# Layer 0's output projection: one FP32 product or three rounded products of high and low parts

## What is computed

```
h = gamma * layernorm(x) + beta                 # gamma, beta from the condition
q, k, v = split(h @ Wqkv.T + bqkv)
att = softmax(q @ k.T) / 512 ** 0.5             # per head, 1024 x 1024
out = (att @ v) @ Wp.T + bp                     # <- the projection, 1024 x 512 x 512 per batch
h1 = out + x
x1 = gamma * layernorm(h1) + beta + h1
```

## Time and profile before

| | |
|---|---|
| median of three runs | 2753.63 us |
| profiled execution, its own time | 2753.1 us |
| its span | 2750.3 us |
| PE busy | 2641.1 us, 96% |
| DVE, ACT, POOL busy | 2148.9, 1837.6, 1963.8 us |
| L997, the projection | 256 MATMULs, 117.3 us busy |
| mean granted TensorE clock | 0.988 of full |

### The profile page before, as it was taken

The page is one execution under the profiler, slowest core; times in us unless marked ns, Lnnn a source line. Parts: engine busy times, 40 slices in busy tenths (PEclk is TensorE's granted clock), DMA queues, the critical chain, the costliest instruction groups (busy, mean ns, idle before and its releaser), DMA issues. The chain is left out here.

```text
span 2750.3 us, 60608 instructions
## 1 busy us (share of the span) xinstructions
PE 2641.1 (96%) x22053; PEld 1488.5 (54%) x22053; DVE 2148.9 (78%) x4445; ACT 1837.6 (67%) x3315; POOL 1963.8 (71%) x1579
## 2 busy tenths in 40 slices
PE   9999999999999999999889999999999999998998
PEld 7655566555765547555445554554455445544443
DVE  5777678776787767877687778777877787758997
ACT  4466665666556665566556677667766776667996
POOL 0399844897459873689759887987889689965442
PEclk9999999999999999999989999999999999999999
DMA  7122353224432335223233214321432232245444
GB/s 238 40 60 59 118 171 105 59 60 151 139 98 59 80 124 170 72 60 105 79 80 82 60 33 120 83 59 36 114 79 60 58 90 60 60 171 178 104 104 111
DMA packets 170351, 260.46 MB, mean 95 GB/s; under 512 B 85436, under 2 KB 93252, under 8 KB 169160
## 3 DMA queue, kind: packets, MB, share of 16 engines
q1 hardware_dynamic: 168264, 250.27, 33.5%
q0 software_dynamic: 1792, 6.33, 0.6%
HBM read 99.15 MB, written 38.88 MB: 50 GB/s over the span
## 5 line engine op out<-in xcount | busy, mean ns | idle before, releaser
L555 DVE TENSOR_REDUCE a_mxs<-ps 128x1 f32<-128x512 f32 x2048 | 1268.6, 683 | 249.5 <-PE ps L420 247.1
L514 ACT ACTIVATE a_p<-ps 128x512 f32<-128x512 f32 x2048 | 1043.8, 605 | 196.7 <-PE ps L434 186.6
L374 POOL TENSOR_TENSOR a_sum<-a_p 128x512 f32<-128x512 f32 x736 | 939.1, 1286 | 196.5 <-PE ps L454 112.7
L420 PE MATMUL ps<-a_k,a_q 96*128 96x512 f32 x2048 | 853.1, 422 | 16.6 <-DVE a_mxs L555 14.6
L434 PE MATMUL ps<-a_q,a_k 98*128 98x512 f32 x2048 | 806.6, 418 | 15.8 <-ACT a_p L514 7.6
L454 PE MATMUL ps<-a_sum,a_unit 128*32 128x512 f32 x1536 | 650.5, 596 | 0.6 <-POOL a_sum L374 0.6
L380 POOL TENSOR_TENSOR a_sum<-a_sum,a_p 128x512 f32<-128x512 f32 x480 | 618.8, 1289 | 37.6
L454 PE MATMUL ps<-a_p,xv 128*32 128x512 f32 x3968 | 638.9, 595 | 0.0
L420 PEld LDWEIGHTS ps<-a_k,a_q 96*128 96x128 f32 x2048 | 386.2, 189 | 252.6 <-DVE a_mxs L555 101.5
L434 PEld LDWEIGHTS ps<-a_q,a_k 98*128 98x128 f32 x2048 | 383.3, 188 | 242.8 <-ACT a_p L514 145.4
L523 ACT ACTIVATE a_ots<-ps 128x512 f32<-128x512 f32 x256 | 152.8, 598 | 403.4 <-PE ps L454 402.3
(11 more groups left out here) (259 smaller groups left out, 3145.0 us busy)
## 6 DMA issues: line engine op xcount, KB each, us to landing
a_q<-qh SPq DMA_DIRECT2D x256, 128.0 KB, 2.3
a_k<-kh SPq DMA_DIRECT2D x256, 128.0 KB, 2.4
a_q<-ql SPq DMA_DIRECT2D x128, 128.0 KB, 2.4
a_k<-kl SPq DMA_DIRECT2D x128, 128.0 KB, 2.4
x<-a_p SPq DMA_DIRECT2D x64, 256.0 KB, 2.5
a_p<-in_w_fc SPq DMA_DIRECT2D x12, 1024.0 KB, 8.1
kh<-in_x SPq DMA_DIRECT2D x4, 2048.0 KB, 14.6
a_p<-x SPq DMA_DIRECT2D x16, 512.0 KB, 6.4
```

The lines of the kernel that those rows point to most:

```text
L374: pair = pool.tensor_tensor(tile, keys[0], keys[1], ALU.add)
L420: pe.matmul(self.mx[self.mx_ring[at]], self.q[j][0:96, t * P:(t + 1) * P], self.k[j][0:96, half * HALF:(half + 1) * HALF], start=True, sto ...
L514: act.activation(self.key_tile(u, kt), self.st[self.st_ring[CHUNKS * k + n]], ACT.Exp, scale=self.scale).then_inc(self.s_exp, 1)
L555: dve.reduce_max(self.mxs[:, k % 2, c:c + 1], self.mx[self.mx_ring[CHUNKS * k + c]], axis=AX.X).then_inc(self.s_mxr, 1)
```

## The change

The FP32 product is replaced by three F32R products (high token by low weight, high by high, low by high), 96 instead of 32 products a batch.

- ACT writes the rounded high part of all eight token groups (`HI_AT`, `high`), DVE subtracts it from PSUM and writes the low part (`LO_AT`, `low`). The low parts go into `q[0]`, `k[0]`, `q[1]`, `k[1]`, whose heads are over by then. These hold rows of ones that the next batch needs (`k[j][96:98]`), so POOL writes them again (`ones_rows`) at the head of each following batch and at the end of layer 0.
- The weight is split once, in batch 0, in head 14: four roundings on ACT, four subtractions on DVE (`WP_AT`). Both parts (2 MB) are written to DRAM behind batch 0's attention, and batches 1 to 3 load them in place of `wp` (2 MB for 1 MB).
- In `late()` the weight comes ahead of `h1`; `mod_r` and `bp` move to `after()`, into the free halves of `q[2]` and `k[2]`.
- SP gets four waits: `s_x1` ahead of the first loads of a batch, the end of head 14's scores in `after()`, `s_wplo` ahead of the write of the parts in batch 0, and, in the last batch, `s_y >= 32` ahead of the loads into `q[0]` and `q[1]`, since these now hold low parts until the projection is done.

```
@@ -142,6 +142,7 @@
     Pending.xq = nc.dram_tensor("xq1", [B, P, TT, D], BF16).ap()
     Pending.dq_row = nc.dram_tensor("dq1_row", [B, T], FP32).ap()
     Pending.dq_col = nc.dram_tensor("dq1_col", [B, P, TT], FP32).ap()
+    Pending.wp_parts = nc.dram_tensor("w0_proj", [P, 2 * KC * D], FP32).ap()
     Pending.w_hi = nc.dram_tensor("w0_hi", [P, 6, T], FP32).ap()
@@ -654,9 +657,12 @@
 
         late = [t[:, :, :].bitcast(FP32).rearrange("p k t -> p (k t)") for t in stage]
         wp = late[0][:, 0:KC * D].rearrange("p (k n) -> p k n", k=KC)
-        mod_r = late[0][:, KC * D:(KC + 2) * D].rearrange("p (i d) -> p i d", i=2)
-        bp = late[0][:, (KC + 2) * D:(KC + 3) * D]
-        oT = late[1].rearrange("p (k t) -> p k t", k=KC)
+        wp_parts = nc.alloc_sbuf_tensor_at("a_wp_parts", [P, 2, KC, D], F32R, offset=Pending.stage_at)
+        wp_all = wp_parts[:, :, :, :].bitcast(FP32).rearrange("p i k n -> p (i k n)")
+        mod_r = nc.alloc_sbuf_tensor_at("a_mod_r", [P, 2, D], FP32, offset=att.q_at + 2 * 4 * T)[:, :, :]
+        bp = nc.alloc_sbuf_tensor_at("a_bp", [P, D], FP32, offset=att.k_at + 2 * 4 * T)[:, :]
+        oT_hi = nc.alloc_sbuf_tensor_at("a_oT_hi", [P, KC, T], F32R, offset=Pending.stage_at + 4 * KC * T)
+        oT_lo = [att.q[0], att.k[0], att.q[1], att.k[1]]
         h1 = late[2].rearrange("p (t d) -> p t d", t=TT)
...
-        COPIED_AT = {(14, 5): 0, (14, 6): 1, (15, 0): 2, (15, 1): 3, (15, 2): 4, (15, 4): 5}
+        HI_AT = {(14, 5): 0, (14, 6): 1, (15, 0): 2, (15, 1): 3, (15, 2): 4, (15, 4): 5}
+        LO_AT = {(14, 6): 0, (14, 7): 1, (15, 1): 2, (15, 2): 3, (15, 3): 4, (15, 5): 5}
+        WP_AT = {(14, 1 + k): k for k in range(KC)}
...
@@ -830,14 +839,19 @@
                     def late():
                         if not last:
                             front(b + 1)
+                        if b == 0:
+                            sp.dma_start(wp, ins["wpT"].rearrange("(k p) n -> p k n", p=P)).then_inc(s_wp, 16)
+                        else:
+                            sp.wait_ge(s_wpout, 16)
+                            sp.dma_start(wp_all, Pending.wp_parts).then_inc(s_wp, 16)
+                        sp.dma_start(h1, x_in[bass.ds(b * T, T), :].rearrange("(t p) d -> p t d", p=P)).then_inc(s_res, 16)
+
+                    def after():
                         sp.wait_ge(s_mout, 16)
-                        sp.dma_start(h1, x_in[bass.ds(b * T, T), :].rearrange("(t p) d -> p t d", p=P)).then_inc(s_res, 16)
-                        sp.dma_start(wp, ins["wpT"].rearrange("(k p) n -> p k n", p=P)).then_inc(s_late, 16)
+                        sp.wait_ge(att.s_st, CHUNKS * (H * b + H - 1) + att.ST_CREDIT)
                         sp.dma_start(mod_r.rearrange("p i d -> p (i d)"),
                                      mod[bass.ds(b, 1), :, :].rearrange("a i d -> a (i d)").broadcast_to([P, 2 * D])).then_inc(s_late, 16)
                         sp.dma_start(bp, rows(ins["bp"], P)).then_inc(s_late, 16)
-
-                    def after():
                         if last:
...
@@ -865,6 +881,7 @@
                     sp.wait_ge(att.s_pv, att.ROUNDS * H // 2 * (b + 1) + att.PV_CREDIT)
                     if last:
                         sp.wait_ge(s_qout, OUTS)
+                        sp.wait_ge(s_y, TT * B)
                         for j in range(2):
                             sp.dma_start(att.q[j][:, :].bitcast(BF16), Pending.xq[0, :, 4 * j:4 * j + 4, :].rearrange("p t d -> p (t d)")).then_inc(s_next, 16)
                     if not last:
@@ -872,6 +889,8 @@
                             load_hi(g)
                         weights(b + 1, (0, 1))
                     if b == 0:
+                        sp.wait_ge(s_wplo, KC)
+                        sp.dma_start(Pending.wp_parts, wp_all).then_inc(s_wpout, 16)
                         sp.wait_ge(s_wout, 32)
                     sp.dma_start(g1.rearrange("p i d -> p (i d)"), rows(mods[1][b, :, :].rearrange("i d -> (i d)"), P)).then_inc(s_g1_in, 16)
...
@@ -887,9 +906,17 @@
                 sp.wait_ge(s_store, 16 * TT * B + 16)
                 sp.wait_ge(s_qout, OUTS * (B - 1) + 16 * 2)
                 sp.wait_ge(s_next, 16 * 4)
+                sp.wait_ge(s_wpout, 16)
 
             @block.gpsimd
             def _(pool):
+                def ones_rows(b):
+                    pool.wait_ge(s_y, TT * b)
+                    pool.wait_ge(s_x1, TT * b + 1)
+                    for j in range(NJ - 1):
+                        pool.memset(att.k[j][96:98, :].bitcast(FP32), 1.0).then_inc(s_rows1, 1)
+                    pool.wait_ge(s_rows1, (NJ - 1) * b)
+
                 pool.memset(unit[:, :], 1.0).then_inc(s_unit, 1)
                 pool.wait_ge(s_unit, 1)
                 att.setup_pool(pool)
@@ -902,6 +929,8 @@
 
                 def batch(b, last):
                     if b:
+                        pool.wait_ge(s_xb, TT * b)
+                        ones_rows(b)
                         shift(b - 1)
...
                     att.run_pool(pool, b)
-                    pool.wait_ge(s_late, 48 * (b + 1))
+                    pool.wait_ge(s_late, 32 * (b + 1))
                     pool.wait_ge(s_res, 16 * (b + 1))
...
                 batches(pool, lambda b: None, batch)
+                pool.wait_ge(s_n2, TT * B)
+                ones_rows(B)
...
@@ -976,25 +1007,29 @@
                     else:
                         pe.wait_ge(att.s_o, 2 * H * (b + 1) + c + 1)
                     if 3 <= i < EARLY:
-                        pe.wait_ge(s_opD, EARLY * b + i - 3 + 1)
+                        pe.wait_ge(s_opD, len(TOKENS) * b + i - 3 + 1)
                     for n in range(4):
                         mm = pe.transpose(ps[:, T_BANK[i], n * P:(n + 1) * P], tok[:, 4 * c + n, k * P:(k + 1) * P], ident)
                     mm.then_inc(s_op, 1)
 
                 def projected(b, t, k):
                     if (t, k) == (0, 0):
-                        pe.wait_ge(s_late, 48 * (b + 1))
+                        pe.wait_ge(s_wp, 16 * (b + 1))
+                        pe.wait_ge(s_wplo, KC)
                     if t < 3 and k == 0:
-                        pe.wait_ge(s_opD, EARLY * b + 3 + t + 1)
+                        pe.wait_ge(s_opD, len(TOKENS) * b + 3 + t + 1)
                     if (t, k) == (3, 0):
                         pe.wait_ge(att.s_exp, CHUNKS * H * (b + 1) + att.EXP_CREDIT)
                     if (t, k) == (4, 0):
-                        pe.wait_ge(s_opD, EARLY * (b + 1))
+                        pe.wait_ge(s_opD, len(TOKENS) * b + EARLY)
                     if t >= 6 and k == 0:
-                        pe.wait_ge(s_opA, 2 * b + t - 6 + 1)
+                        pe.wait_ge(s_opD, len(TOKENS) * b + t + 1)
                     if t in (0, 4) and k == KC - 1:
-                        pe.wait_ge(s_opA, 2 * b + t // 4 + 1)
-                    mm = pe.matmul(ps[:, Y_BANK[t], :], oT[:, k, t * P:(t + 1) * P], wp[:, k, :], start=k == 0, stop=k == KC - 1)
+                        pe.wait_ge(s_opD, len(TOKENS) * b + EARLY + t // 4 + 1)
+                    hi, lo = oT_hi[:, k, t * P:(t + 1) * P], oT_lo[k][:, t * P:(t + 1) * P]
+                    pe.matmul(ps[:, Y_BANK[t], :], hi, wp_parts[:, 1, k, :], start=k == 0, stop=False)
+                    pe.matmul(ps[:, Y_BANK[t], :], hi, wp_parts[:, 0, k, :], start=False, stop=False)
+                    mm = pe.matmul(ps[:, Y_BANK[t], :], lo, wp_parts[:, 1, k, :], start=False, stop=k == KC - 1)
                     if k == KC - 1:
                         mm.then_inc(s_y, 1)
...
                         act.activation(xn[:, t, :], xn[:, t, :], ACT.Identity, bias=nmx[:, t:t + 1], scale=rs[0][:, t:t + 1]).then_inc(s_z, 1)
-                    att.run_act(act, b, upper=lambda: act.wait_ge(s_wout, 16 * (2 + done(b + 1) - done(1))))
+                    def high(i):
+                        k, c = TOKENS[i]
+                        act.wait_ge(s_op, len(TOKENS) * b + i + 1)
+                        act.activation(oT_hi[:, k, c * HALF:(c + 1) * HALF], ps[:, T_BANK[i], :], ACT.Copy).then_inc(s_opA, 1)
+
+                    def extra(k, s):
+                        if b == 0 and (k, s) in WP_AT:
+                            act.wait_ge(s_wp, 16)
+                            i = WP_AT[k, s]
+                            act.activation(wp_parts[:, 1, i, :], wp[:, i, :], ACT.Copy).then_inc(s_wphi, 1)
+                        if (k, s) in HI_AT:
+                            high(HI_AT[k, s])
+                    att.run_act(act, b, extra, upper=lambda: act.wait_ge(s_wout, 16 * (2 + done(b + 1) - done(1))))
                     if not last:
                         roots(b + 1)
                     for i in range(EARLY, len(TOKENS)):
-                        k, c = TOKENS[i]
-                        act.wait_ge(s_op, len(TOKENS) * b + i + 1)
-                        act.activation(oT[:, k, c * HALF:(c + 1) * HALF], ps[:, T_BANK[i], :], ACT.Copy).then_inc(s_opA, 1)
+                        high(i)
...
```

(30 more changed lines are left out.)

## The result

The median went from 2753.17 to 2772.18 us (four runs each, 2747.51 to 2754.06 and 2769.88 to 2775.72): the ratio is 1.0074, with a 95% interval of [1.0061, 1.0086]. The change made the kernel slower by 19.0 us. The forecast was +24.7, 2777.8; the result lies inside its range, 5.6 us under the forecast. The profiled execution of after took 2769.88 us, of before 2753.1. Two executions of this document, one of e11 and one of the kernel before, took over 4990 us in a slower state and are in no median here.

The account below looks back on a forecast made before the run. ACT's list was taken to bound the first three tails and g1's arrival the last; +20.3 us for the last tail plus small terms made +24.7, so 2753.1 became 2777.8 us, range 2768 to 2785.

Parts of the forecast that it names:

- The smaller terms: Ahead of the last tail: nmx +1.4, high parts +1.2, weight split +1.0, DMAs -1.5 and +0.6, clock +1.7 us.
- The last tail: Last batch: g1 queues behind SP's wait for s_y, so DVE starts 20.9 us later; +20.3 us net.
- rival 3: Last tail: DVE and POOL close up from 35.0 to about 29.84 us, total about 2747 us; chance 0.03.
- The two small waits and the rows of ones: Last tail: DVE's two small waits for PE vanish, -0.6 us; POOL's rewritten rows of ones are covered, zero.
- PE's saving in the first three tails, zero: Tails of batches 0 to 2: shorter products save nothing, since ACT's list is full.
- The 5.2 us named for each tail: Tails of batches 0 to 2: up to 5.2 us less in each if ACT were not the bound.
- nmx: Batches 0 to 2, behind the attention: two low parts ahead of nmx delay ACT's statistics 0.45 us each, +1.4 us.
- High parts in heads 14 to 16, and the split of the weight: Added ACT and DVE work: high parts in heads 14 and 15, +1.2 us; batch 0's weight split, +1.0 us.
- DMAs: Batch 0's wait for head 14's row goes, -1.5 us; larger loads in batches 1 and 2, +0.6; 2 MB write, zero.
- The clock: Behind batch 0's tail: longer PE idle time lowers TensorE's clock for two groups of four products, +1.7 us.
- The products: Projection on PE: three F32R products take 0.69 us in place of one FP32 product's 0.865.

Follow-up runs that it names:

- e11: e10 with five in place of three added F32R products for each of token tiles 3 to 7 in batches 0 to 2; 2746.95 us, ratio 0.9985.
- e1: The changed kernel with the load of g1 in the last batch issued ahead of SP's wait for s_y; 2747.72 us, ratio 0.9991.
- e2: The kernel before plus only SP's last-batch wait for all 32 finished token tiles ahead of its loads into q[0] and q[1]; 2776.2 us, ratio 1.0097.
- e6: The kernel before with most of two weight sums on ACT left out in the tails of batches 0 to 2; 2743.99 us, ratio 0.9981.
- e9: The kernel before with g1 loaded early in the last batch and two weight sums moved from ACT to DVE; 2749.31 us, ratio 1.0001.
- e3: e1 with one F32R product (high by high) in place of three, the two with a low part left out; 2739.55 us, ratio 0.9961.
- e5: e1 with most of two weight sums on ACT left out in the tails of batches 0 to 2; 2741.98 us, ratio 0.9963.
- e4: e1 with DVE computing rs and nmx ahead of the last two low parts; 2750.55 us, ratio 0.9999.
- e10: e4 with three extra F32R products, later overwritten, for each of token tiles 3 to 7 in batches 0 to 2; 2745.0 us, ratio 0.9979.
- e7: e4 with two sums of absolute weight values moved in full from ACT to DVE; 2748.69 us, ratio 0.9999.

## Why the prediction was right

The mechanism was the one forecast, and what carried it, +20.9 to the start of the last tail, measured right. The smaller terms were mostly not: +4.4 forecast ahead of the last tail, +0.19 measured. Some luck helped the total: 1.5 us too little at the tail's end cancels part of that.

**The last tail.** The step that carried the forecast held to a tenth: +20.9 expected from the last token transpose to DVE's first addition, +20.96 measured, `s_y` forecast complete at 1361.1 against 1361.28 for SP's next issue. e1 takes the wait out of `g1`'s way and the whole cost is gone; e2 puts it into the kernel before and the cost is there, without any rounded product. The tail behind it stayed at 35 us: rival 3, which needed DVE and POOL to close up to some 30, is refuted.

**The two small waits and the rows of ones** (-0.6 and 0 in the forecast): together +0.93 instead. POOL's chain of additions gained nothing; it ends 35.26 us behind DVE's first addition in after, 34.90 before. And the rows of ones were not hidden at the end. The end of the last tail in after:

```profile
1403.21 2.80 POOL L917 MEMSET a_k<- 2x1024 f32 x3
1403.90 0.28 DVE L1430 TENSOR_SCALAR am<-am 128x8 f32<-128x8 f32 x1
1404.22 0.20 DVE L1432 RECIPROCAL am<-am 128x8 f32<-128x8 f32 x1
1404.34 0.76 DVE L1433 TENSOR_SCALAR am<-am,dws 128x8 f32<-128x8 f32 x1
1404.46 0.66 DVE L1435 TENSOR_SCALAR am<-am 128x8 f32<-128x8 f32 x1
1405.13 0.32 SPq L834 DMA_DIRECT2D dq_col<-am  x1
```

and the same instructions in the kernel before, where POOL has nothing to do at that time:

```profile
1382.72 0.18 DVE L1384 TENSOR_SCALAR am<-am,dws 128x8 f32<-128x8 f32 x1
1382.84 0.17 DVE L1386 TENSOR_SCALAR am<-am 128x8 f32<-128x8 f32 x1
1382.93 0.32 SPq L825 DMA_DIRECT2D dq_col<-am  x1
```

From DVE's first 128x8 scalar (1382.39 before) to SP's issue it is 0.54 us before and 1.23 after. I had named DMA receipts as the cover, and the memsets do end beside them; what I left out was that DVE's last scalars run at the same time. That is +0.7 of the 0.93. No run took the memsets away alone, but the runs divide by them: the first of the two scalars takes 0.76 or 0.77 us in all eight kernels that have them and 0.18 in all four that don't (before, e2, e6, e9). e2 has the late tail without the memsets, so the late tail is not the cause.

**PE's saving in the first three tails, zero**: shown. 23.39 to 23.40 us in all three of after, with 4.1 us less work on PE, and 23.38 to 23.39 in e3 with 11 us less. e5 and e6 show why: only once ACT's list is shorter does PE's length come through. The 5.2 us named for each tail were too many by the prediction's own numbers: 24 products stand behind the last transpose, and 24 x 0.175 = 4.2.

**nmx** (+0.45 each, +1.4 in all): +1.16 measured, and e4 undoes it.

**High parts in heads 14 to 16, and the split of the weight** (+1.2 and +1.0): these were sized wrong. The stretch measured +0.92 in batch 0 and -0.49 to -0.72 in the others, -0.80 in all for +2.2. I had put the gain of the shorter projections at 0.2 to 0.3 us a batch, since three of the seven "run while POOL makes a sum", and the cost at a high part of ACT's that delays a score. The traces show both otherwise. Eight projections lie in the stretch and are 0.15 to 0.175 us shorter each, 1.2 to 1.4 us; e3 says that some seven tenths of such length count, about 1.0 (an estimate). The cost is a wait that I didn't have: the fifth group of token transposes needs the PSUM bank that DVE's low part frees, and DVE waits for ACT's high part. Here are this wait in batches 0 and 1 of after (the last two lines) and above them the two waits that only batch 0 has, for exponentials that stand behind ACT's roundings of the weight:

```profile
314.73 0.50 PE L437 MATMUL ps<-a_q,a_k 98*128 98x512 f32 x1 [0.21 <-ACT a_p L517]
316.33 0.50 PE L437 MATMUL ps<-a_q,a_k 98*128 98x512 f32 x1 [0.42 <-ACT a_p L517]
323.46 0.63 PE L1012 MATMUL ps<-ident,tok 128*128 128x128 f32 x4 [0.96 <-DVE a_k L1577]
657.45 0.63 PE L1012 MATMUL ps<-ident,tok 128*128 128x128 f32 x4 [0.58 <-DVE a_k L1577]
```

Before, PE has no wait in these stretches. In batches 1 and 2 the 0.58 against the 1.0 gained gives about the -0.5 measured; batch 3 has no such wait and should have gained more than its 0.72, which stays open. Of the 1.4 us that batch 0 has more than batches 1 and 2, the two waits and the longer third make 1.0; that is the split of the weight. The Trainium skill (Perfetto Trace Analysis, Identifying the Most-Contended Engine) would have PE, the engine of the highest occupancy, optimized first, with its reservation for TensorE's busy time; the runs agree with it in these rounds, by 2.6 us a batch in e3, and disagree in the tails, where the same edit moved 0.01 us.

**DMAs.** The wait of 1.50 us for head 14's row in batch 0 is gone, and the stretch is 1.14 shorter (forecast 1.5); three of the four roundings of the weight start in it too. The larger loads of batches 1 and 2 cost nothing that the waits show: PE waits 0.49 us for that row in batch 1 and none in batch 2, 0.63 and 1.15 before. The stretches from q to the tokens in the three later batches are 0.48 us shorter together, for +0.6. What the write of 2 MB costs, forecast at zero, no run shows by itself.

**The clock** (+1.7): from the last x transposes to the third q group it takes 3.24, 4.79 and 4.80 us in the kernel before, and 4.83, 4.80 and 5.61 in after. That is +2.4, of which +1.74 stands in the table's row and the rest in the one below it. Batch 0 costs 1.6, as charged; that batch 2's fall would last 0.8 us longer I had not foreseen. A part of this is chance: in e2, whose tails have the same code and the same idle time, batch 2 kept the full clock that before lost (3.22 for 4.80 us).

**The products**: three start 0.68 us apart, 0.69 forecast. The Trainium skill (FP8 and Floating Point Precision, TensorE Precision Notes) counts four passes for true FP32, by which three would take three quarters, an estimate of 0.65 us. The measured 0.68 is 0.79 of the 0.865, nearer to the 0.69 of the rows.

So of the 5.6 us between forecast and median, the stages ahead of the last tail account for 4.2 (+4.4 forecast, +0.19 measured), mostly heads 14 to 16 (3.0 of them); the tail's end goes 1.5 the other way, and the rest is the spread between executions, of which layer 1's 4.4 us is an example.

## What to carry to other kernels

A wait added to a queue that issues in order costs what is queued behind it: look for the first transfer behind it that somebody waits for, and put that one ahead if it doesn't need the wait; here one moved line gave back some 23 us. Before shortening the busiest engine's work, look stage by stage whose list is full: PE was busy 96% of the span, and in the tails even two thirds of the projection's products, left out, gave nothing while ACT's list was full. When a rounding step is put between a copy and the next user of its PSUM bank, ask who waits for the bank. Work "hidden" beside a DMA should also be looked at for the small instructions of another engine that lie under it.

## What the runs showed of the hardware

**The same idle time did and did not cost the clock.** Each of the twelve profiled kernels has three tails that end with PE idle before its last x transposes. Here they are sorted by that idle time, with the time from those transposes to the third group of q products. At full clock that is 3.2 us; everything longer is the lower level.

```
idle before    tails (kernels)                            full clock    fell, us to the third group
1.26 - 1.54     9  (e5, e6, e11)                              9          -
1.87 - 1.92     7  (before, e2, e10)                          3          4: 4.79 to 4.86
2.17 - 2.25     6  (before, e2, e7, e9)                       2          4: 4.80 to 5.23
2.33 - 3.74    14  (after, e1, e3, e4, e7)                    0         14: 4.66 to 5.93
```

In the second and third row the same program fell in one batch and not in another: before's batches 0 and 1 did so at 1.90 us both. The idle time just ahead of the transposes alone doesn't tell which; what else does stays open. Most falls cost 1.6 us, e4's three 2.7 each.

**DVE's smallest instructions are stretched beside POOL's memsets.** Two 128x8 scalars took 0.76 and 0.66 us where they take 0.18 and 0.17 without, in eight kernels with the memsets and four without.

**The tails are exact.** Over after, e1, e3, e4 and e10 their length from DVE's first addition varies between 23.38 and 23.42 us, while layer 1's 1360 us of the same code vary by almost 6 us between the twelve profiled executions. A difference of a few tenths can be read from a stage where the median of the kernel can't show it.
